# Expert layer: the two slots of a token summed in front of the down-projection

## The chip, the cores and the metric

The kernel runs on one core of one Trainium2 chip. The metric is the device time of one execution in microseconds (us). Lower is better.

## The reference, cut to what matters

One decoder layer on 64 images of 128 tokens and 128 channels: causal self-attention, cross-attention to 77 context tokens, and a mixture of experts with a residual. The change touches only the last part. A token goes to its two best experts of eight ("slots" 0 and 1 here). Each expert differs from the others only by low-rank terms (rank 16, so 8 x 16 = 128 rows for all experts together).

```python
probs = softmax(x @ gate_w.T);  vals, idx = top_k(probs, 2)
rw = vals / sum(vals)                                   # the two gates of a token, w0 + w1 = 1
act_e = silu(x @ w_gate.T + d1_e) * (x @ w_up.T + d3_e) # 512 wide; d1_e, d3_e of rank 16, x2
out = sum_e w_e * act_e @ w_down.T
z_e = act_e @ A2_e.T                                    # 16 wide
out = out + sum_e w_e * (z_e @ B2_e.T) * 2
x = x + out
```

## The kernel before, in words

X holds all 64 images on chip, tokens on the partitions. Three stages follow one another with a layer norm's statistics in front of each: self-attention, cross-attention, `expert_ffn`. Matrix products of the experts are made of three products each of high and low parts in a rounded f32 format (`three`): high x high, high x low, low x high.

**Experts.** `expert_ffn` works on G = 32 groups of NB = 2 images (256 tokens, NT = 256 columns). Each engine runs its own list of steps, `step(g, p)`, one per group, in an order written out by hand; semaphores join them. Every engine executes its own list strictly in order. In step g the engines do, for group g, four units: k = 0, 1 are the halves of the 512 hidden channels for slot 0, k = 2, 3 those for slot 1. Two PSUM banks each (H1, H3) hold the gate and up products of a half; slot 1's products are accumulated on slot 0's, so that its 24 matmuls per unit shrink to 12.

- TensorE (`up`, `down`): `up(g, k)` makes a unit, `down(g, k)` (lines 1793 to 1795) multiplies its result with the down-projection and A2 side by side: the gated activations are the weights, 128 tokens of them at a time, and the 256 columns of w_down and A2 are streamed, so that the outputs have tokens on the partitions. It has 2 x 2 x 3 = 12 matmuls per unit for all four units. Units 2 and 3 of group g-1 are done in step g, as k = -2 and -1. `z_T` (line 1803) transposes the low-rank result of both images, `extra` (lines 1726 to 1728, 6 matmuls of 128 columns) multiplies it with B2. `input_T`, `logits`, `a_products`, `masks` prepare the groups that follow.
- ScalarE: `silu` (1526), `g_hi` (1531, high part of the gated activation), `z_hi` (1536); for the groups that follow `normalise`, `input_T`, `a_hi`, `spread` (one-hot picks widened), `masks` (1504, the two slots' expert masks to SBUF), `gate_odds` (the gates w0 and w1 by a tanh, as [128, 2] each).
- VectorE: `gated` (1640, silu x up, one operand in PSUM), `g_lo` (1645, low part, both operands in SBUF), `x_lo` (1583), `a_lo`, `ranks` and `picks` (top 2 of 8 in small operations), `slot_weights` (1633), `slot_z` (1655, low-rank result times expert mask and gate), `residual_y` (1664, four operations of 128 columns: X + gate x Y), `z_lo` (1671), `residual_z` (1676).
- GpSimd: `slot_sum` (1458, 256 columns) of group g-1, then `slot_inputs` (1466) of group g+1: four products of 512 columns, two for each slot, of the low-rank inputs and the expert mask.
- SyncE stores the two images of a group as soon as `x_done` tells.

The order of VectorE in a step is `residual_z(g-2)`, `x_lo(g+1)`, `ranks(g+1)`, `slot_weights(g)`, `gated 0`, `g_lo 0`, `a_lo(g+1)`, `picks(g+1)`, `gated 1`, `slot_z(g-1)`, `g_lo 1`, `residual_y(g-1)`, `gated 2`, `gated 3`, `z_lo(g-1)`, `g_lo 2`, `g_lo 3`. Of ScalarE it is silu 0, g_hi 0, a_hi, normalise, spread, silu 1, g_hi 1, masks(g+1), silu 2, silu 3, z_hi(g-1), g_hi 2, g_hi 3, input_T(g+2), gate_odds(g+1).

Of the kernel before, what the change touches and what calls it, by code (L numbers as in the profile page):

```python
# [69 lines left out]
def inverse_std(nc, tag, X, ST, MEAN, RSTD, with_stats, load_more=None):  # L70
# [3 lines left out]
    with ctx:  # L74
# [4 lines left out]
        loaded = [ctx.enter_context(nc.semaphore(f"{tag}_loaded{g}")) for g in range(4)]  # L79
# [1254 lines left out]
def expert_ffn(nc, psum, X, MEAN, RSTD, hi, lo, plain, out_dram):  # L1334
# [13 lines left out]
    RANKED, ROUTE = 8, 13  # L1348
    ctx = ExitStack()
    with ctx:  # L1350
# [33 lines left out]
        zt = sb("zt", [128, NB, 2, C])  # L1384
        zz = sb("zz", [128, NB, C])
# [56 lines left out]

        @block.sync
        def _(sp):
            with sp.Fori(0, G) as g:
# [5 lines left out]
            sp.wait_ge(stored, 16 * B)

        @block.gpsimd
        def _(pool):
            def slot_sum(g):
                pool.wait_ge(zt_done, NB * g + NB)
                need(pool, zT_ps, g)
                nc.gpsimd.tensor_tensor(zz[:], zt[:, :, 0, :], zt[:, :, 1, :], ALU.add).then_inc(zz_done, 1)  # L1458

            def slot_inputs(g, p):  # L1460
                pool.wait_ge(mask_sb, g + 1)
                for s in range(2):
                    for part, done in enumerate((ah_done, al_done)):
                        pool.wait_ge(done, g + 1)
                        need(pool, up_ps, UNITS * (g - 2) + 2 * s + 2)
                        nc.gpsimd.tensor_tensor(ZZ[part][:, p, s], AA[part][:].bitcast(F32),  # L1466
                                                M[:, s, :].unsqueeze(1).to_broadcast([C, 2, NT]),
                                                ALU.mult).then_inc(z_done, 1)
# [466 lines left out]
```

## Time and profile before

| | us |
|---|---|
| median of three runs (1767.62 to 1772.02) | 1767.89 |
| profiled execution, its own time | 1771.94 |
| its span, first to last instruction | 1770.1 |
| TensorE busy | 1641.4 (93%) |
| VectorE busy | 1232.2 (70%) |
| ScalarE busy | 924.0 (52%) |
| GpSimd busy | 880.6 (50%) |

Busy times are sums over the whole span; the span of the profiled execution lies 1.8 us below its own time, and that is 4.05 us above the median. The experts' stage starts at 1213.8 us. In its profile one step of the experts repeats with the same order of instructions for all groups but the first and the last, so that one step can be read for all of them. A matmul's duration is longer than its share of the queue, since matmuls are pipelined: what one costs is read from start to start. The same holds, less strongly, for VectorE and ScalarE.

### The profile page before, as it was taken

Reading aid. Unit: us, or ns where it says so; the run is one execution under the profiler, and the core shown is the slowest. Engines: PE = TensorE matmul, PEld = TensorE weight load, DVE = VectorE, ACT = ScalarE, POOL = GpSimd, SP = SyncE. Lnnn points to the kernel's source line nnn. Section 1 sums busy time; section 2 is a strip of 40 time slices with the busy share of each in tenths; the row PEclk is TensorE's granted clock in tenths of the full one; section 3 lists DMA queues with packets and bytes.
Section 4 is the critical chain, followed back from the end, with each engine's and each line's share of the span. In section 5 each row is a group of like instructions: output and inputs, shape, how many; then the busy total and the mean of one; then the engine's idle time right before and its main releaser. Section 6 shows DMA issues by size and latency. Waiting matters only on the chain. (4 is left out here: it accounts for less than half of the span.)

```text
span 1770.1 us, 42709 instructions
## 1 busy us (share of the span) xinstructions
PE 1641.4 (93%) x14274; PEld 1231.9 (70%) x14336; DVE 1232.2 (70%) x2839; ACT 924.0 (52%) x2183; POOL 880.6 (50%) x977
## 2 busy tenths in 40 slices
PE   0899999999977899999999999995999999999998
PEld 0455555555545666666666666555999999999998
DVE  4577777777755667776767767615787887887876
ACT  1345455445443566665666666644545555454453
POOL 0444444444426676776776767621343343443442
PEclk9999999999996899998999989987999999999999
DMA  6000000000000000000000000000000000000000
GB/s 170 2 2 1 1 1 1 1 1 1 1 7 6 4 7 6 7 7 6 7 7 6 7 6 7 2 2 1 8 8 7 9 6 9 9 6 9 9 6 13
DMA packets 26456, 16.60 MB, mean 9 GB/s; under 512 B 6194, under 2 KB 23667, under 8 KB 26355
## 3 DMA queue, kind: packets, MB, share of 16 engines
q1 hardware_dynamic: 26354, 15.29, 3.1%
q8 instruction: 59, 0.97, 0.2%
q14 instruction: 43, 0.34, 0.1%
HBM read 10.03 MB, written 4.19 MB: 8 GB/s over the span
## 5 line engine op out<-in xcount | busy, mean ns | idle before, releaser
L293 ACT ACTIVATE sa_P<-sa_SK 128x1024 f32<-128x1024 f32 x128 | 131.4, 1027 | 150.8 <-PE sa_SK L438 150.8
L1458 POOL TENSOR_TENSOR ff_zz<-ff_zt 128x256 f32<-128x256 f32 x32 | 38.4, 1199 | 319.4 <-DVE ff_zt L1655 319.4
L250 POOL TENSOR_TENSOR sa_KM<-sa_HQK,sc_headmask 128x512 fp32r<-128x512 f32 x64 | 66.6, 1041 | 245.7 <-ACT sa_HQK L288 245.7
L865 ACT ACTIVATE xa_P<-xa_SK 77x1024 f32<-77x1024 f32 x128 | 130.1, 1017 | 98.0 <-PE xa_SK L1157 97.7
L1526 ACT ACTIVATE ff_SG<-bank 128x512 f32<-128x512 f32 x128 | 76.8, 600 | 192.5 <-PE bank L1728 192.5
L1645 DVE TENSOR_TENSOR ff_GL<-ff_GU,ff_GH 128x512 fp32r<-128x512 f32 x128 | 147.7, 1173 | 27.4 <-ACT ff_GH L1531 27.1
L366 DVE TENSOR_REDUCE sa_mx<-sa_SQ 128x8 f32<-128x1024 f32 x128 | 156.6, 1223 | 11.1 <-PE sa_SQ L438 8.3
L1793 PE MATMUL bank<-fh_r,ff_GH 128*128 128x256 f32 x512 | 148.2, 290 | 0.0
L1726 PE MATMUL bank<-ff_ZH,fh_b 128*128 128x256 f32 x512 | 147.8, 289 | 0.0
L791 POOL TENSOR_TENSOR xa_QMH<-xa_QBH,xc_headmask 128x512 fp32r<-128x512 f32 x64 | 72.8, 1138 | 148.2 <-ACT xa_QBH L855 148.1
L1727 PE MATMUL bank<-ff_ZL,fh_b 128*128 128x256 f32 x512 | 145.1, 283 | 0.0
L1728 PE MATMUL bank<-ff_ZH,fl_b 128*128 128x256 f32 x512 | 145.0, 283 | 0.0
L1795 PE MATMUL bank<-fh_r,ff_GL 128*128 128x256 f32 x512 | 143.5, 280 | 0.0
L750 POOL TENSOR_TENSOR xa_E<-xa_E 128x1232 f32<-128x1232 f32 x64 | 143.2, 2238 | 0.0
L1794 PE MATMUL bank<-fl_r,ff_GH 128*128 128x256 f32 x512 | 142.9, 279 | 0.0
L1640 DVE TENSOR_TENSOR ff_GU<-ff_SG,bank 128x512 f32<-128x512 f32 x128 | 88.0, 687 | 68.9 <-ACT ff_SG L1526 63.5
L1531 ACT CAST ff_GH<-ff_GU 128x512 fp32r<-128x512 f32 x128 | 78.9, 623 | 55.3 <-DVE ff_GU L1640 32.2
L1466 POOL TENSOR_TENSOR ff_ZH<-ff_AH,ff_M 128x512 fp32r<-128x512 f32 x64 | 83.7, 1308 | 41.5 <-ACT ff_M L1504 41.5
L962 DVE TENSOR_REDUCE xa_FEAT<-xa_SQ 128x12 f32<-128x924 f32 x64 | 71.7, 1120 | 41.8 <-PE xa_SQ L1106 41.6
L457 PE MATMUL sa_SK<-sa_shift,sa_pick_row 128*128 128x512 f32 x256 | 99.7, 470 | 0.2 <-ACT sa_P L293 0.2
L1726 PEld LDWEIGHTS bank<-ff_ZH,fh_b 128*128 128x128 f32 x512 | 98.5, 192 | 0.0
L1727 PEld LDWEIGHTS bank<-ff_ZL,fh_b 128*128 128x128 f32 x512 | 98.5, 192 | 0.0
(259 smaller groups left out, 5381.2 us busy)
## 6 DMA issues: line engine op xcount, KB each, us to landing
xa_shift<-xa_row SPq DMA_DIRECT2D x256, 2.0 KB
out<-X SPq DMA_DIRECT2D x64, 64.0 KB, 1.5
xa_cx<-ctx SPq DMA_DIRECT2D x64, 38.5 KB
sa_shift<-sa_mT SPq DMA_DIRECT2D x64, 8.0 KB, 1.8
fr_b<-L_ffn_B SPq DMA_DIRECT2D x2, 256.0 KB, 3.9
fr_r<-down_a SPq DMA_DIRECT2D x1, 512.0 KB, 4.7
fr_w<-L_ffn_w_gate SPq DMA_DIRECT2D x1, 256.0 KB, 3.5
fr_w<-L_ffn_w_up SPq DMA_DIRECT2D x1, 256.0 KB, 3.6
```

The source lines that it names most:

```text
L293: nc.scalar.activation(P[:, 2 * (k % 2) + h, :], SK[:], ACT.Exp).then_inc(p_ready, 1)
L366: nc.vector.tensor_reduce(mx[:, p, 2 * JH * h:2 * JH * h + 2 * JH], SQ[:].rearrange("q (j k) -> q j k", k=T), AX.X, ALU.max).then_inc(max_ ...
L457: mm(bank(SK, a), pick_row[:], shift[:, k % 2, JH * g:JH * g + JH, :].rearrange("c j t -> c (j t)"), start=True, stop=False)
L750: nc.gpsimd.tensor_tensor(E2[:], E1[:, b % 2], E1[:, b % 2], ALU.mult).then_inc(e2_ready, 1)
L865: nc.scalar.activation(P[0:TC, (2 * b + h) % 4, :], SK[0:TC, :], ACT.Exp).then_inc(p_ready, 1)
L1645: nc.vector.tensor_tensor(GG[1][:, k % 4, :], GU[:, k % 2, :], GG[0][:, k % 4, :].bitcast(F32), ALU.subtract).then_inc(gl_done, 1)
L1726: mm(out, w[0], x[0], start=start, stop=False, **kw)
L1727: mm(out, w[0], x[1], start=False, stop=False, **kw)
L1728: return mm(out, w[1], x[0], start=False, stop=stop, **kw)
L1793: mm(out, h, RD[0][:, f, :], start=(s == 0 and f == 0), stop=False, skip_group_check=True)
L1794: mm(out, h, RD[1][:, f, :], start=False, stop=False, skip_group_check=True)
L1795: last = mm(out, l, RD[0][:, f, :], start=False, stop=(s == 1 and f == 3), skip_group_check=True)
```

## The change

The sum of a token's two slots is taken on the gated activations, w0 (act0 + (w1/w0) act1), so that the down-projection proper runs once for both; w0 is applied at the residual. The low-rank part needs the slots apart by expert: PZ holds A2 x act0 and A2 x (act0 + ratio x act1), and the masks ME = (mask1, mask0 + mask1 - mask0) pick out the parts, whose difference goes on. The matrices are now the weights and the activations (256 tokens) are streamed, so outputs have channels on the partitions and are transposed back at the end (`back_T`).

TensorE: `down` has 6 matmuls of 256 columns for k = 0, 1 and 12 for k = 2, 3; `extra` has 3 of 256 columns; `z_T` is gone; `ratios` (two f32 products of 128 columns, which lay the ratio across the partitions) and `back_T` (two transposes) are new. ScalarE: `ratio_copy` and `out_copy` are new, `z_hi` moves between silu 2 and silu 3. VectorE: `odds` (reciprocal and product, [128, 2]), two `slot_sum` of 512 columns, two `z_parts` of 256 columns, two `residual` of 128 columns in place of `slot_weights`, `slot_z`, `residual_y` and `residual_z`; `z_lo` reads SBUF alone and stands in front of `gated 2`. GpSimd: two `scaled` of 512 columns (silu of slot 1 times the ratio, in place), which `gated` 2 and 3 wait for, two `output_masks` and a `z_sum` of 256 columns, and `slot_inputs` of slot 0 stands in front of `z_sum`.

```diff
-def slot_inputs(g, p):
+def slot_inputs(g, p, s):
     pool.wait_ge(mask_sb, g + 1)
...
+def output_masks(g, p):
+    pool.wait_ge(mask_sb, g + 1)
+    need(pool, zb_done, 2 * (g - 1))
+    nc.gpsimd.tensor_tensor(ME[:, p, 1], M[:, 0, :], M[:, 1, :], ALU.add).then_inc(me_done, 1)
+    pool.wait_ge(me_done, 2 * g + 1)
+    nc.gpsimd.tensor_tensor(ME[:, p, 0], ME[:, p, 1], M[:, 0, :], ALU.subtract).then_inc(me_done, 1)
+def scaled(g, u):
+    pool.wait_ge(rb_sb, g + 1)
+    pool.wait_ge(silu_done, UNITS * g + 2 + u + 1)
+    unit2 = SG[:, u, :].rearrange("f (c n) -> f c n", c=2)
+    nc.gpsimd.tensor_tensor(unit2, unit2, RB[:].unsqueeze(1).to_broadcast([128, 2, NT]),
+                            ALU.mult).then_inc(scaled_done, 1)
+def z_sum(g):
+    pool.wait_ge(zb_done, 2 * g + 2)
+    need(pool, zl_done, g)
+    nc.gpsimd.tensor_tensor(zs[:], zb[:, 1, :], zb[:, 0, :], ALU.subtract).then_inc(zs_done, 1)
 def step(g, p):
+    if real(g + 1):
+        slot_inputs(g + 1, 1 - p, 0)
     if real(g - 1):
-        slot_sum(g - 1)
+        z_sum(g - 1)
+    scaled(g, 0)
+    scaled(g, 1)
     if real(g + 1):
-        slot_inputs(g + 1, 1 - p)
+        slot_inputs(g + 1, 1 - p, 1)
+        output_masks(g + 1, 1 - p)
...
+def ratio_copy(g):
+    act.wait_ge(rb_ps, g + 1)
+    need(act, scaled_done, 2 * g)
+    nc.scalar.copy(RB[:], BF[:, NT:2 * NT]).then_inc(rb_sb, 1)
 def silu(g, k):
     act.wait_ge(up_ps, UNITS * g + k + 1)
...
     nc.scalar.activation(SG[:, k % 2, :], H1[k % 2][:], ACT.Silu).then_inc(silu_done, 1)
 def g_hi(g, k):
-    act.wait_ge(gu_done, UNITS * g + k + 1)
+    if k < 2:
+        act.wait_ge(gu_done, UNITS * g + k + 1)
+    else:
+        act.wait_ge(sum_done, 2 * g + k - 1)
     need(act, y_ps, UNITS * g + k - 3)
-    nc.scalar.copy(GG[0][:, k % 4, :], GU[:, k % 2, :]).then_inc(gh_done, 1)
+    nc.scalar.copy(GG[0][:, k, :], GU[:, k % 2, :]).then_inc(gh_done, 1)
 def z_hi(g):
-    act.wait_ge(zT_ps, g + 1)
-    need(act, extra_ps, g)
-    nc.scalar.copy(ZT[0][:], BS[:, 0:NT]).then_inc(zh_done, 1)
+    act.wait_ge(zs_done, g + 1)
+    need(act, out_ps, g)
+    nc.scalar.copy(ZT[0][:], zs[:]).then_inc(zh_done, 1)
+def out_copy(g):
+    act.wait_ge(out_ps, g + 1)
+    need(act, back_ps, g)
+    nc.scalar.copy(OT[:], OUT[:, 0:NT]).then_inc(out_sb, 1)
 def step(g, p):
     silu(g, 0)
...
         normalise(g + 2)
     if real(g + 1):
         spread(g + 1)
+    ratio_copy(g)
     silu(g, 1)
     g_hi(g, 1)
     if real(g + 1):
         masks(g + 1)
     silu(g, 2)
-    silu(g, 3)
     if real(g - 1):
         z_hi(g - 1)
+    silu(g, 3)
+    if real(g + 2):
+        input_T(g + 2, p)
+    if real(g - 1):
+        out_copy(g - 1)
     g_hi(g, 2)
     g_hi(g, 3)
-    if real(g + 2):
-        input_T(g + 2, p)
     if real(g + 1):
-        gate_odds(g + 1, 1 - p)
+        gate_odds(g + 1)
...
+def odds(g):
+    dve.wait_ge(w0_ready, g + 1)
+    nc.vector.reciprocal(w0_inv[:], W0[:, bass.ds(NB * g, NB)]).then_inc(inv_ready, 1)
+    dve.wait_ge(inv_ready, g + 1)
+    dve.wait_ge(w1_ready, g + 1)
+    need(dve, rb_ps, g)
+    nc.vector.tensor_tensor(ratio[:], w1[:], w0_inv[:], ALU.mult).then_inc(ratio_ready, 1)
 def gated(g, k):
-    dve.wait_ge(silu_done, UNITS * g + k + 1)
+    if k < 2:
+        dve.wait_ge(silu_done, UNITS * g + k + 1)
+    else:
+        dve.wait_ge(scaled_done, 2 * g + k - 1)
     need(dve, gl_done, UNITS * g + k - 1)
-    nc.vector.tensor_tensor(GU[:, k % 2, :], SG[:, k % 2, :], H3[k % 2][:], ALU.mult).then_inc(gu_done, 1)
+    out = GU if k < 2 else G1
+    nc.vector.tensor_tensor(out[:, k % 2, :], SG[:, k % 2, :], H3[k % 2][:], ALU.mult).then_inc(gu_done, 1)
+def slot_sum(g, u):
+    dve.wait_ge(gu_done, UNITS * g + 2 + u + 1)
+    nc.vector.tensor_tensor(GU[:, u, :], GU[:, u, :], G1[:, u, :], ALU.add).then_inc(sum_done, 1)
 def g_lo(g, k):
     dve.wait_ge(gh_done, UNITS * g + k + 1)
     need(dve, y_ps, UNITS * g + k - 3)
-    nc.vector.tensor_tensor(GG[1][:, k % 4, :], GU[:, k % 2, :], GG[0][:, k % 4, :].bitcast(F32),
+    nc.vector.tensor_tensor(GG[1][:, k, :], GU[:, k % 2, :], GG[0][:, k, :].bitcast(F32),
                             ALU.subtract).then_inc(gl_done, 1)
-def slot_z(g, p):
+def z_parts(g, p):
     dve.wait_ge(y_ps, UNITS * g + UNITS)
...
+    dve.wait_ge(me_done, 2 * g + 2)
+    need(dve, zs_done, g)
+    for part in range(2):
+        nc.vector.tensor_tensor(zb[:, part, :], PZ[:, part * NT:(part + 1) * NT], ME[:, p, part],
+                                ALU.mult).then_inc(zb_done, 1)
 def z_lo(g):
     dve.wait_ge(zh_done, g + 1)
...
+    need(dve, out_ps, g)
+    nc.vector.tensor_tensor(ZT[1][:], zs[:], ZT[0][:].bitcast(F32), ALU.subtract).then_inc(zl_done, 1)
+def residual(g):
+    dve.wait_ge(back_ps, g + 1)
+    for n in range(NB):
+        xb = X[:, bass.ds((NB * g + n) * C, C)]
+        nc.vector.scalar_tensor_tensor(xb, OUT[:, NT + n * C:NT + (n + 1) * C], W0[:, bass.ds(NB * g + n, 1)], xb,
+                                       ALU.mult, ALU.add).then_inc(x_done, 1)
 def step(g, p):
     if real(g - 2):
-        residual_z(g - 2)
+        residual(g - 2)
+    odds(g)
     if real(g + 1):
         x_lo(g + 1, 1 - p)
         ranks(g + 1)
-    slot_weights(g, p)
     gated(g, 0)
     g_lo(g, 0)
     if real(g + 1):
         a_lo(g + 1)
         picks(g + 1)
     gated(g, 1)
-    if real(g - 1):
-        slot_z(g - 1, 1 - p)
     g_lo(g, 1)
     if real(g - 1):
-        residual_y(g - 1, 1 - p)
+        z_parts(g - 1, 1 - p)
+        z_lo(g - 1)
     gated(g, 2)
+    slot_sum(g, 0)
     gated(g, 3)
-    if real(g - 1):
-        z_lo(g - 1)
+    slot_sum(g, 1)
     g_lo(g, 2)
     g_lo(g, 3)
...
+def ratios(g):
+    pe.wait_ge(ratio_ready, g + 1)
+    if real(g + 1):
+        pe.wait_ge(route, ROUTE * (g + 1) + 1)
+    for n in range(NB):
+        last = mm(BF[:, NT + n * T:NT + (n + 1) * T], ratio[:, n:n + 1].to_broadcast([128, 128]), ident[:],
+                  start=True, stop=True, skip_group_check=True)
+    last.then_inc(rb_ps, 1)
 def down(g, k):
-    if not unit(g, k):
+    if not real(g):
         return
-    s, u = divmod(k % UNITS, 2)
+    u = k % 2
     pe.wait_ge(gl_done, UNITS * g + k + 1)
     if k == 0:
-        need(pe, zt_done, NB * g)
-        need(pe, y_step, 4 * g)
+        need(pe, zb_done, 2 * g)
+    if k == 2:
+        need(pe, x_done, NB * g)
     for c in range(2):
         f = 2 * u + c
...
+        unit = [t[:, k, c * NT:(c + 1) * NT] for t in GG]
+        at = k // 2 * NT
+        last = three(PZ[:, at:at + NT], [t[:, f, C:2 * C] for t in RD], unit, f == 0, f == 3, skip_group_check=True)
+        if k >= 2:
+            last = three(OUT[:, 0:NT], [t[:, f, 0:C] for t in RD], unit, f == 0, False, skip_group_check=True)
     last.then_inc(y_ps, 1)
...
 def extra(g):
     pe.wait_ge(zh_done, g + 1)
     pe.wait_ge(zl_done, g + 1)
+    last = three(OUT[:, 0:NT], [t[:] for t in B2], [t[:] for t in ZT], False, True, skip_group_check=True)
+    last.then_inc(out_ps, 1)
+def back_T(g):
+    pe.wait_ge(out_sb, g + 1)
     for n in range(NB):
-        last = three(BS[:, NT + n * C:NT + (n + 1) * C],
-                     [t[:, n * T:(n + 1) * T] for t in ZT], [t[:] for t in B2], True, True)
-    last.then_inc(extra_ps, 1)
+        last = tr(OUT[:, NT + n * C:NT + (n + 1) * C], OT[:, n * T:(n + 1) * T], ident[:])
+    last.then_inc(back_ps, 1)
 def step(g, p):
     up(g, 0, p)
-    down(g, -2)
+    down(g - 1, 2)
     if real(g + 1):
         a_products(g + 1, 1 - p)
+    ratios(g)
     up(g, 1, p)
-    down(g, -1)
     if real(g + 1):
         masks(g + 1)
+    down(g - 1, 3)
     up(g, 2, p)
     up(g, 3, p)
-    if real(g - 1):
-        z_T(g - 1)
-    down(g, 0)
     if real(g + 2):
         input_T(g + 2)
-    down(g, 1)
+    down(g, 0)
     if real(g - 1):
         extra(g - 1)
+    down(g, 1)
     if real(g + 2):
         logits(g + 2)
+    if real(g - 1):
+        back_T(g - 1)
```

## Rows read from the trace of the kernel before

**Rows 1.** Page: the span; part 1, busy us, share and count of each engine.
```profile
span 1770.1 us, 42709 instructions
...
PE 1641.4 (93%) x14274; PEld 1231.9 (70%) x14336; DVE 1232.2 (70%) x2839; ACT 924.0 (52%) x2183; POOL 880.6 (50%) x977
```

**Rows 2.** Time windows: length, busy us (count) of each engine, granted clock.
```profile
484.00:528.00 44.00, 34.53 (x341) 19.71 (x341) 25.75 (x63) 18.53 (x37) 12.85 (x16) 0.94 0.02 5
528.00:572.00 44.00, 34.77 (x148) 24.58 (x148) 22.03 (x42) 15.74 (x51) 25.69 (x34) 0.59 0.02 7
1475.60:1492.40 16.80, 16.80 (x147) 16.76 (x145) 13.39 (x34) 8.55 (x19) 6.68 (x6) 1.00 0.03 8
```

**Rows 3.** Chain of waits, experts stage: start us, us, what.
```profile
1257.22 0.39 PE bank L1740 x4
...
1727.62 0.39 PE bank L1740 x4
```

**Rows 4.** Timeline of TensorE, experts: start us, us, engine, line, what.
```profile
1474.84 0.22 PE L1726 MATMUL bank<-fh_b,ff_ZTH 128*128 128x128 f32 x1
...
1475.45 0.56 PE L1740 MATMUL bank<-fc_gw,ff_xT 128*128 128x8 f32 x4
...
1478.82 0.28 PE L1793 MATMUL bank<-fh_r,ff_GH 128*128 128x256 f32 x1
...
1480.22 0.28 PE L1726 MATMUL bank<-ff_XH,fh_a 128*128 128x256 f32 x1
```

**Rows 5.** Timeline of TensorE in cross-attention: one f32 product, then another's start.
```profile
707.54 0.49 PE L1092 MATMUL xa_M<-xa_xcT,xc_wq 128*128 128x128 f32 x2
707.87 0.34 PE L1093 MATMUL xa_M<-xa_xcT,xc_wk 128*128 128x77 f32 x2
```

**Rows 6.** Timeline of VectorE, one step; in brackets idle before it, releaser.
```profile
1476.61 0.41 DVE L1676 TENSOR_TENSOR X<-X,bank 128x256 f32 x1
1476.94 0.41 DVE L1583 TENSOR_TENSOR ff_XL<-ff_xT,ff_XH 128x256 fp32r<-128x256 f32 x1
...
1479.21 0.17 DVE L1633 TENSOR_TENSOR ff_V<-ff_pick,ff_wt 128x16 f32<-128x16 f32 x1
...
1479.82 0.69 DVE L1640 TENSOR_TENSOR ff_GU<-ff_SG,bank 128x512 f32<-128x512 f32 x1 [0.34 <-ACT ff_SG L1526]
...
1485.42 0.75 DVE L1655 TENSOR_TENSOR ff_zt<-bank,ff_V 128x256 f32<-128x256 f32 x2
1486.19 0.69 DVE L1645 TENSOR_TENSOR ff_GL<-ff_GU,ff_GH 128x512 fp32r<-128x512 f32 x1
1486.80 1.25 DVE L1664 SCALAR_TENSOR_TENSOR X<-bank,ff_wt,X 128x128 f32 x4
...
1490.15 3.31 DVE L1645 TENSOR_TENSOR ff_GL<-ff_GU,ff_GH 128x512 fp32r<-128x512 f32 x2
```

**Rows 7.** Timeline of ScalarE, the same step.
```profile
1479.10 0.60 ACT L1526 ACTIVATE ff_SG<-bank 128x512 f32<-128x512 f32 x1 [4.20 <-PE bank L1728]
...
1485.97 0.58 ACT L1504 CAST ff_M<-bank 128x512 f32<-128x512 bf16 x1
```

**Rows 8.** Timeline of GpSimd, the same step.
```profile
1486.25 1.22 POOL L1458 TENSOR_TENSOR ff_zz<-ff_zt 128x256 f32<-128x256 f32 x1 [10.12 <-DVE ff_zt L1655]
1487.44 1.29 POOL L1466 TENSOR_TENSOR ff_ZH<-ff_AH,ff_M 128x512 fp32r<-128x512 f32 x1
1488.68 1.30 POOL L1466 TENSOR_TENSOR ff_ZL<-ff_AL,ff_M 128x512 fp32r<-128x512 f32 x1
...
1491.20 1.72 POOL L1466 TENSOR_TENSOR ff_ZL<-ff_AL,ff_M 128x512 fp32r<-128x512 f32 x1
```

**Rows 9.** Timeline of VectorE, last step of the experts.
```profile
1757.28 1.28 DVE L1645 TENSOR_TENSOR ff_GL<-ff_GU,ff_GH 128x512 fp32r<-128x512 f32 x2
```

**Rows 10.** Groups of instructions, shapes apart: count, busy us, mean ns, idle before.
```profile
L256 POOL TENSOR_TENSOR sa_QML<-sa_LQK,sc_headmask 128x512 fp32r<-128x512 f32 x64 | 66.6, 1041 | 0.0
...
L375 DVE RECIPROCAL sa_rinv<-sa_R 128x16 f32<-128x16 f32 x64 | 15.9, 248 | 4.9 <-PE sa_R L498 4.9
```

More of the change, by code:

```diff
@@ L78, in inverse_std @@
         t = ctx.enter_context(nc.sbuf_tensor(tag + "_t", [128, B], F32))
-        loaded = [ctx.enter_context(nc.semaphore(f"{tag}_loaded{g}")) for g in range(4)]
+        loaded = [ctx.enter_context(nc.semaphore(f"{tag}_loaded{g}")) for g in range(4 if with_stats is not None else 0)]
         gathered = ctx.enter_context(nc.semaphore(tag + "_gathered"))
@@ L1383, in expert_ffn @@
         GG = [sb("GH", [128, 4, 2 * NT], F32R), sb("GL", [128, 4, 2 * NT], F32R)]
[L1384 to L1385 removed]
+        G1 = sb("G1", [128, 2, 2 * NT])
+        zb = sb("zb", [128, 2, NT])
+        zs = sb("zs", [128, NT])
+        OT = sb("OT", [C, NT])
         ZT = [sb("ZTH", [C, NT], F32R), sb("ZTL", [C, NT], F32R)]
@@ L1400, in expert_ffn @@
         th_ready = sem("th_ready")
-        wt_ready = sem("wt_ready")
-        v_ready = sem("v_ready")
+        w0_ready = sem("w0_ready")
+        w1_ready = sem("w1_ready")
+        inv_ready = sem("inv_ready")
+        ratio_ready = sem("ratio_ready")
+        rb_ps = sem("rb_ps")
+        rb_sb = sem("rb_sb")
+        scaled_done = sem("scaled_done")
+        sum_done = sem("sum_done")
+        me_done = sem("me_done")
         mask_ps = sem("mask_ps")
@@ L1445, in _ @@
             with sp.Fori(0, G) as g:
-                sp.wait_ge(x_done, g + 1)
+                sp.wait_ge(x_done, NB * g + NB)
                 for n in range(NB):
@@ L1454, in _ @@
         def _(pool):
[L1455 to L1458, printed above, removed]
-            def slot_inputs(g, p):
-                pool.wait_ge(mask_sb, g + 1)
[L1462 to L1468, printed above, removed]
+            def slot_inputs(g, p, s):
+                pool.wait_ge(mask_sb, g + 1)
+                for part, done in enumerate((ah_done, al_done)):
+                    pool.wait_ge(done, g + 1)
+                    need(pool, up_ps, UNITS * (g - 2) + 2 * s + 2)
+                    nc.gpsimd.tensor_tensor(ZZ[part][:, p, s], AA[part][:].bitcast(F32),
+                                            M[:, s, :].unsqueeze(1).to_broadcast([C, 2, NT]),
+                                            ALU.mult).then_inc(z_done, 1)
@@ L1473, in step, with first @@
                 if real(g + 1):
-                    slot_inputs(g + 1, 1 - p)
-            groups(pool, lambda: slot_inputs(0, 0), step, lambda: slot_sum(G - 1))
+                    slot_inputs(g + 1, 1 - p, 1)
+                    output_masks(g + 1, 1 - p)
+            def first():
+                slot_inputs(0, 0, 0)
+                slot_inputs(0, 0, 1)
+                output_masks(0, 0)
+            groups(pool, first, step, lambda: z_sum(G - 1))
         @block.scalar
@@ L1710, in end @@
             def end():
-                residual_z(G - 2)
-                slot_z(G - 1, 1)
-                residual_y(G - 1, 1)
+                residual(G - 2)
+                z_parts(G - 1, 1)
                 z_lo(G - 1)
-                residual_z(G - 1)
-                dve.wait_ge(x_done, G)
+                residual(G - 1)
+                dve.wait_ge(x_done, NB * G)
             groups(dve, first, step, end)
@@ L1745, in a_products @@
                 pe.wait_ge(xl_ready, g + 1)
-                need(pe, x_done, g - 2)
                 for m in range(2):
@@ L1844, in end @@
             def end():
-                down(G, -2)
-                down(G, -1)
-                z_T(G - 1)
+                down(G - 1, 2)
+                down(G - 1, 3)
                 extra(G - 1)
+                back_T(G - 1)
             groups(pe, first, step, end)
```

83 lines of the change are left out of this document (21 added, 62 removed).

## The prediction

> **What bounds the kernel now.** I read the page's busy shares first: TensorE is busy 93% of the span, the next engine 70% [rows 1]. Over a whole span that says little, so I went to the window of one step in the experts' stage: TensorE is busy 16.80 of 16.80 us at full clock, VectorE 13.39, ScalarE 8.55, GpSimd 6.68 [rows 2]. The chain of waits confirms the period: the same piece of TensorE's work returns at 1257.22 and at 1727.62, 470.4 us or 28 steps of 16.80 [rows 3]. So the experts' stage is bound by TensorE's queue, and each step has slack of 3.4 us on VectorE. How that slack is made up is in the timelines. They show no spare room that is free of waits: VectorE works its list in order, and stands before `gated 0` only 0.34 us [rows 6].
>
> **TensorE's part, alone.** Twelve matmuls of one old `down` take from 1478.82 to 1480.22, 1.40 us or 0.117 each [rows 4]. `down` goes from 48 to 36 of them: -1.40 us. `extra` takes 0.61 us for its 6 matmuls of 128 columns [rows 4]; 3 of 256 columns take 0.35: -0.26. `z_T` is replaced by `back_T`, two transposes for two: 0. `ratios` is new: one f32 product of 128x128 takes 0.33 us from start to start [rows 5], two take +0.66. Sum -1.0 us, a period of 15.8 us, if nothing else held TensorE.
>
> **What the port costs.** In the old step `g_lo 2` and `g_lo 3` together take 3.31 us while GpSimd's products run, and 1.28 in the last step, where GpSimd has none [rows 6, 9]. One of them, in the queue, is 0.61 us: `g_lo 1` from 1486.19 to 1486.80 [rows 6]. GpSimd pays as well: its product beside them takes 1.72 where an undisturbed one goes from 1487.44 to 1488.68, 1.24 [rows 8]. And its `slot_sum`, starting at 1486.25, just behind `g_lo 1`, and ending where the next begins at 1487.44, moved only once `g_lo 1` was through at 1486.80: its own work is 0.64 us [rows 6, 8]. All of it fits turns taken instruction by instruction. From 1490.15 the pair waits for the product until 1491.20, runs 0.61, waits for the next product's 1.24, runs 0.61: 3.51 against 3.31 shown. `gated`, with an operand in PSUM, does not pay. The Trainium skill (SBUF — State Buffer, "Who interferes with whom") states the rule: a VectorE instruction with two SBUF inputs and a GpSimd instruction that reads SBUF exclude each other for a whole instruction. It speaks against this change, which adds such instructions on both sides; a shared bandwidth instead would stretch both and leave no turns.
>
> GpSimd's own work in a step grows from 4 x 1.24 + 0.64 = 5.6 to 4 + 2 products of 1.24 and three operations of 0.64, 9.4 us. For the products I take 1.24 also for `scaled`; another such product elsewhere takes 1.04 [rows 10], which is the low bound. The Trainium skill (GPSIMD Engine Reference, "Elementwise — side-by-side cycle accounting") gives 2.6 cycles an element for two inputs, an estimate of 1.1 us for 512; with it the forecast would be about 9 us lower. VectorE gains two `slot_sum` of 0.61 with both operands in SBUF, and `z_lo` becomes one of them too.
>
> **The ring.** What decides is order. VectorE runs its list strictly in order, GpSimd too, and the change makes them wait for each other three times in a step. I walk from the start of `gated 0` of one step to that of the next.
> - A: `gated 0` to the first product of GpSimd. Between are g_hi 0, g_lo 0, picks, spread, silu 1, gated 1, g_hi 1 and the copy of the masks, which GpSimd's whole list for the step waits for. Before, `gated 0` starts at 1479.82 [rows 6] and the copy ends at 1486.55 [rows 7]: 6.7, with 0.1 for the handoff 6.8 us. (A handoff: the silu ends at 1479.70, `gated 0` starts at 1479.82 [rows 6, 7].) `ratio_copy` adds work on ScalarE in front of silu 1, but silu 1 waited for TensorE there before; taken as 0.
> - B: GpSimd's chain, with VectorE's turns between. Two products for slot 0, 2.48. Then only `z_sum`, 0.64. `z_parts` (0.75, as `slot_z` [rows 6]) was ready long before and lies beside the products. z_hi (ScalarE) and then `z_lo` (VectorE) come behind `z_sum`, and in the meantime GpSimd has begun `scaled 0`, 1.24: `z_lo` gets the port after it, 0.33 (as `residual_z`, 1476.61 to 1476.94 [rows 6]). All of VectorE's list stands behind that `z_lo`: it is idle from the end of `z_parts` for some 3.5 us. Then in turn: `scaled 1` 1.24 (`gated 2` beside it), slot sum 0.61, product 1.24 (`gated 3` beside it), slot sum 0.61, product 1.24, g_lo 2 0.61, an output mask 0.64, g_lo 3. Sum without the last: 7.44 + 1.28 + 0.33 + 1.83 = 10.9 us.
> - C: g_lo 3 0.61, `residual` 2 x 0.31 (four such took 1.25 [rows 6]), `odds` 0.45 (a reciprocal of 16 columns took 0.25 [rows 10], a [128, 16] product 0.17 [rows 6]), `x_lo` and `ranks` 2.27 (1476.94 to 1479.21 [rows 6]). Sum 3.95 us. The old V products are gone from here.
>
> A + B + C = 21.7 us a step, against 16.8. TensorE with 15.8 us of work has 5.9 us of idle time in it and its own waits lie inside: in front of `down` of the last group's unit 2 it waits for `residual` (x_done, which stands behind g_lo 3), and before `extra` for `z_lo`. With `extra` waiting, unit 1's `down`, `logits`, `back_T` and the next group's first `up` stand behind it, but that `up` ends some 2 us before the ring needs its silu. ScalarE's silu 3 stands behind z_hi, which costs nothing as `scaled 1` waits for the port anyway. The stores on SyncE follow `x_done` and are hidden as before, but for the last.
>
> **The sum.** 31 periods between the first and the last `gated 0`, each 4.9 us longer: +152. The first step has no low-rank result of a group before it (-1), the last step's chain of slot sum, z_sum, z_hi, z_lo, extra, copy and transpose is longer by about as much: 0. The profiled execution took 1771.94 us by its own time, 1.8 more than its span of 1770.1 [rows 1]; so 1924, and as it lies 4.05 above the median of the three runs, 1920 against 1767.89.
>
> **Bounds of this case.** `scaled` at 1.04 and everything else of GpSimd's 256 columns in proportion: 0.6 less a step, 1901. If each of some twelve handoffs of 0.12 us shows behind the turns: +1.4 a step, 1963.
>
> **Rivals.**
> 1. *The order binds, but the port does not, or only in part.* For it: turns may fall luckier than I walk them. Against it: g_lo's pair at 3.31 us in the steps with GpSimd and 1.28 without [rows 6, 9]. Then B shrinks: s0 and z_sum end at 9.8 us, scaled 0 and gated 2 at 11.8, gated 3 at 13.0, the second slot sum 13.65, g_hi 3, g_lo 3 at 15.1, rest of C 3.35: 18.5 us a step, 31 x 1.7 = +53, 1821. Mixed cases lie up to 1900.
> 2. *Faster: TensorE stays the bound.* Place: TensorE's queue from `up 0` to `up 0`. Price: 15.8 instead of 16.8 us, 32 steps, -32: 1736. It decides only if the ring of the two other engines closes in under 15.8 us. For it: TensorE is the bound now and its work does shrink. Against: even without the port the ring takes 18.5.
> 3. *The clock falls.* Now a step runs at clock 1.00. TensorE would stand idle in stretches of up to 2.7 us, 5.9 of each 21.7. In cross-attention's start, with 34.77 us busy of 44, the clock was 0.59; just before it with 34.53 of 44 it was 0.94 [rows 2]. So both can be had near such shares. At 1.2 GHz a step of matmuls would take some 31 us, which closes the gaps again; half of the steps so gives 26.6 us, +304, 2072.
> 4. *No change in time*, the ring closing at 16.8 just as TensorE's work did: only a coincidence of 1 and 2.
>
> **How the numbers follow.** Ring with turns, 1901 to 1963: 0.72. Rival 1: 0.15. Rival 2: 0.06. Rival 3: 0.05. Rival 4: 0.02. The likeliest gives 1920. The range takes in its bounds and most of rival 1: 1835 to 1965. What a measurement here can tell from no change is about 0.3%, 5 us. Faster by more than that 0.06, same 0.02, slower 0.92.
>
> **What would show it.** A period of 21 to 22.5 us between the same instructions of two steps. In VectorE's timeline an idle stretch of 3 us or more before `z_lo`, ended by ScalarE's z_hi, itself behind GpSimd's `z_sum`; slot sums of more than 1 us and a `g_lo 2` near 1.8; GpSimd busy without a hole from the masks' copy to the output masks; TensorE busy near three quarters, with waits for X and for ZTL; the window's clock at 1.00. Wrong would be: `z_lo` without idle time before it, TensorE busy throughout, or slot sums of 0.69 beside running `scaled` (then the port is not what I take it for).

## The result and the profile after

The changed kernel takes 1902.95 us (median of four runs, 1900.55 to 1908.83) against 1768.88 for the kernel of before beside it: a ratio of 1.076, 95% interval 1.073 to 1.079. Slower, inside the range of 1835 to 1965, 17 us under the 1920 forecast. The last of the reordered kernels (experiments 6 to 10 below) brings the same arithmetic to 1760.34 us, 0.5% under the kernel of before, which took 1768.21 beside it.

The page first. Beside [rows 1], TensorE's share fell from 93% to 87%, and the chain of waits, which was TensorE's alone through the experts, is now spread over VectorE, ScalarE, GpSimd and the handoffs between them ("issue" is time in which an engine waited for nothing that the profile shows). The third line below is that chain of waits, as shares of the span.

```profile
span 1900.8 us, 42609 instructions
...
PE 1652.0 (87%) x13984; PEld 1224.2 (64%) x13984; DVE 1267.8 (67%) x2775; ACT 943.2 (50%) x2247; POOL 1033.0 (54%) x1105
...
issue 12%; DVE 12%; ACT 4%; PE 3%; POOL 2%; DVEq 1%; ACTq 0%; POOLq 0%
```

Windows of the experts' stage (as [rows 2]: length, busy us (count) of TensorE, its weight loads, VectorE, ScalarE, GpSimd, granted clock, DMA share, GB/s):

```profile
1276.40:1297.30 20.90, 15.89 (x133) 15.36 (x132) 14.51 (x31) 9.15 (x21) 11.26 (x10) 1.00 0.03 7
1351.20:1372.80 21.60, 19.49 (x134) 19.27 (x134) 14.49 (x32) 9.26 (x21) 11.43 (x9) 0.80 0.02 6
1519.40:1540.40 21.00, 17.04 (x144) 16.52 (x143) 14.52 (x31) 9.23 (x21) 11.49 (x9) 1.00 0.02 6
1255.00:1856.00 601.00, 491.46 (x3810) 476.88 (x3809) 417.79 (x890) 261.90 (x601) 331.39 (x260) 0.94 0.02 6
```

VectorE's timeline over one step, from `gated 0` at 1519.43 to the next at 1540.42, 20.99 us; it stands beside [rows 6]. To be seen: 2.98 us idle in front of `z_lo` (ZTL), slot sums (L1695) of 1.07 and 1.08, the pair of `g_lo` at 2.92 (1.78 and 1.21, which overlap by 0.08).

```profile
1519.43 0.69 DVE L1691 TENSOR_TENSOR ff_GU<-ff_SG,bank 128x512 f32<-128x512 f32 x1 [0.22 <-DVE ff_rank L1659]
...
1526.22 0.75 DVE L1709 TENSOR_TENSOR ff_zb<-bank,ff_ME 128x256 f32<-128x256 f32 x2
1529.95 0.95 DVE L1715 TENSOR_TENSOR ff_ZTL<-ff_zs,ff_ZTH 128x256 fp32r<-128x256 f32 x1 [2.98 <-ACT ff_ZTH L1576]
1530.83 0.67 DVE L1691 TENSOR_TENSOR ff_G<-ff_SG,bank 128x512 f32<-128x512 f32 x1
1531.54 1.07 DVE L1695 TENSOR_TENSOR ff_GU<-ff_GU,ff_G 128x512 f32<-128x512 f32 x1
1532.53 0.67 DVE L1691 TENSOR_TENSOR ff_G<-ff_SG,bank 128x512 f32<-128x512 f32 x1
1533.24 1.08 DVE L1695 TENSOR_TENSOR ff_GU<-ff_GU,ff_G 128x512 f32<-128x512 f32 x1
1534.23 2.92 DVE L1700 TENSOR_TENSOR ff_GL<-ff_GU,ff_GH 128x512 fp32r<-128x512 f32 x2
1537.08 0.59 DVE L1721 SCALAR_TENSOR_TENSOR X<-bank,ff_W,X 128x128 f32 x2
...
1540.42 0.69 DVE L1691 TENSOR_TENSOR ff_GU<-ff_SG,bank 128x512 f32<-128x512 f32 x1 [0.21 <-DVE ff_rank L1659]
```

GpSimd's timeline of the same step (beside [rows 8]): from the masks' copy to the output mask it has no hole. Undisturbed products start 1.27 and 1.24 apart; the two that alternate with slot sums take 1.69 and 1.73 from their own start to that of the next.

```profile
1526.16 1.31 POOL L1469 TENSOR_TENSOR ff_ZH<-ff_AH,ff_M 128x512 fp32r<-128x512 f32 x1 [9.33 <-ACT ff_M L1538]
1527.43 1.28 POOL L1469 TENSOR_TENSOR ff_ZL<-ff_AL,ff_M 128x512 fp32r<-128x512 f32 x1
1528.67 0.74 POOL L1491 TENSOR_TENSOR ff_zs<-ff_zb 128x256 f32<-128x256 f32 x1
1529.37 2.69 POOL L1485 TENSOR_TENSOR ff_SG<-ff_SG,ff_RB 128x512 f32<-128x512 f32 x2
1532.02 1.74 POOL L1469 TENSOR_TENSOR ff_ZH<-ff_AH,ff_M 128x512 fp32r<-128x512 f32 x1
1533.71 1.75 POOL L1469 TENSOR_TENSOR ff_ZL<-ff_AL,ff_M 128x512 fp32r<-128x512 f32 x1
1535.44 1.17 POOL L1477 TENSOR_TENSOR ff_ME<-ff_M 128x256 f32<-128x256 f32 x1
```

The waits of the whole run (who waited for whom, us in total, times, longest) name the chain through `z_sum`, z_hi and `z_lo`, and TensorE behind it:

```profile
DVE ff_ZTL L1715 <- ACT ff_ZTH L1576: 90.6, 32, 3.0
...
ACT ff_ZTH L1576 <- POOL ff_zs L1491: 65.5, 32, 7.6
...
PE bank L1770 <- DVE ff_ZTL L1715: 56.4, 32, 2.6
...
PE bank L1770 <- DVE X L1721: 41.0, 27, 3.4
```

**Where the time is.** The first `gated 0` starts at 1227.91, the last at 1872.46: 31 steps of 20.79 us. Before, 1230.45 and 1747.78 give 16.69. That is 31 x 4.10 = 127 us. The tail behind the last `gated 0` is 28.3 us against 22.3, the start 2.5 shorter: 127 + 6.0 - 2.5 = 130.7, the whole difference of the spans (1900.8 and 1770.1). The 2.5 us are not the change's: cross-attention, whose code is the same, ends 2.6 us earlier in this execution (1201.2 and 1203.8). In the twelve profiled executions of this document the first `gated 0` starts anywhere from 1220.2 to 1234.2 us, so a difference of a few us between two executions is better read from the steps than from the totals.

The steps of the changed kernel are not all alike. Most take 20.8 to 20.9 us; four, with a mean clock of 0.80, take 21.5 to 21.6 (1351.2 to 1372.8 is one). Steps at a clock of 0.92 take no more than those at 1.00. So the clock cost some 3 of the 127 us.

### The profile page after: what moved, and what is told of

Same layout as the page of the kernel before. It is cut to its first block and busy times, and to the rows that moved or that the text cites. A ratio compares the mean times of both kernels' runs of the same rounds, so it can differ in the third digit from the quotient of the medians.

```text
span 1900.8 us, 42609 instructions
## 1 busy us (share of the span) xinstructions
PE 1652.0 (87%) x13984; PEld 1224.2 (64%) x13984; DVE 1267.8 (67%) x2775; ACT 943.2 (50%) x2247; POOL 1033.0 (54%) x1105
## 5 line engine op out<-in xcount | busy, mean ns | idle before, releaser
L1469 POOL TENSOR_TENSOR ff_ZH<-ff_AH,ff_M 128x512 fp32r<-128x512 f32 x64 | 96.9, 1515 | 320.9 <-ACT ff_M L1538 320.9
L1700 DVE TENSOR_TENSOR ff_GL<-ff_GU,ff_GH 128x512 fp32r<-128x512 f32 x128 | 135.9, 1080 | 53.1 <-ACT ff_GH L1571 34.3
L1770 PE MATMUL bank<-ff_GH,fh_r 128*128 128x256 f32 x384 | 117.8, 307 | 42.3 <-DVE X L1721 41.0
L1771 PE MATMUL bank<-ff_GL,fh_r 128*128 128x256 f32 x384 | 110.2, 287 | 0.0
L1772 PE MATMUL bank<-ff_GH,fl_r 128*128 128x256 f32 x384 | 110.2, 287 | 0.0
L1770 PEld LDWEIGHTS bank<-ff_GH,fh_r 128*128 128x128 f32 x384 | 74.3, 194 | 47.6 <-DVE ff_GL L1700 29.4
L1772 PEld LDWEIGHTS bank<-ff_ZH,fl_b 128*128 128x128 f32 x512 | 99.8, 195 | 0.0
```

What stands on the lines that cost most here:

```text
L1700: nc.vector.tensor_tensor(GG[1][:, k, :], GU[:, k % 2, :], GG[0][:, k, :].bitcast(F32), ALU.subtract).then_inc(gl_done, 1)
L1770: mm(out, w[0], x[0], start=start, stop=False, **kw)
L1771: mm(out, w[0], x[1], start=False, stop=False, **kw)
L1772: return mm(out, w[1], x[0], start=False, stop=stop, **kw)
```

## The experiments

"After" means the changed kernel; differences are to its 1903 us.

**1. z_lo later.** VectorE's wait moved behind the second slot sum:

```diff
                     z_parts(g - 1, 1 - p)
-                    z_lo(g - 1)
                 gated(g, 2)
                 slot_sum(g, 0)
                 gated(g, 3)
                 slot_sum(g, 1)
+                if real(g - 1):
+                    z_lo(g - 1)
```

> VectorE's z_lo is moved behind the second slot sum, so that nothing of VectorE's list stands behind it while it waits for GpSimd and ScalarE. In the changed kernel VectorE idles 2.9 us a step in front of z_lo. Theory A (the ring of GpSimd's chain): gated 2 waits for scaled 0, which ends at about the same moment as z_lo does now, so the idle time moves in front of gated 2 and the step stays at 20.9 us or gains 0.5 for one more turn at the port: 1900 to 1925 us. Theory B (the wait of z_lo itself is what costs): 2.9 us a step less, 31 steps, about 1815 us.

Measured 2016.73 us, 114 more. VectorE's timeline:

```profile
1519.53 0.69 DVE L1691 TENSOR_TENSOR ff_GU<-ff_SG,bank 128x512 f32<-128x512 f32 x1 [1.91 <-ACT ff_SG L1563]
...
1531.38 0.69 DVE L1691 TENSOR_TENSOR ff_G<-ff_SG,bank 128x512 f32<-128x512 f32 x1 [3.68 <-POOL ff_SG L1485]
...
1534.71 1.48 DVE L1715 TENSOR_TENSOR ff_ZTL<-ff_zs,ff_ZTH 128x256 fp32r<-128x256 f32 x1
1538.28 1.29 DVE L1700 TENSOR_TENSOR ff_GL<-ff_GU,ff_GH 128x512 fp32r<-128x512 f32 x2 [2.08 <-ACT ff_GH L1571]
...
1544.32 0.69 DVE L1691 TENSOR_TENSOR ff_GU<-ff_SG,bank 128x512 f32<-128x512 f32 x1 [1.21 <-ACT ff_SG L1563]
```

The idle time did move: `gated 2` now starts 11.85 us behind `gated 0` (11.40 before) and is released by GpSimd's `scaled`. That part is as theory A had it, and theory B falls. What A's number left out is the queue behind another wait: ScalarE has `out_copy` in front of g_hi 2 and 3, `out_copy` waits for `extra`, and `extra` for `z_lo`. ScalarE's timeline shows the copy of OT at 1537.36, and both high parts only behind it:

```profile
1537.36 0.37 ACT L1581 COPY ff_OT<-bank 128x256 f32<-128x256 f32 x1 [5.53 <-PE bank L1773]
1537.62 1.14 ACT L1571 CAST ff_GH<-ff_GU 128x512 fp32r<-128x512 f32 x2
```

VectorE's pair of `g_lo` waits 2.08 us for them. From the pair's end to the next `gated 0` it takes 1.4 us more than after as well: `gated 0` waits 1.21 us for silu 0, and that for TensorE. The step of these rows takes 24.79 us, the mean one 24.34. So the time lies far outside both theories' numbers, 92 us over the top of A's range. TensorE's clock fell as well, to a mean of 0.90 over the run and 0.79 to 0.86 in nearly every step; how much of the 114 us is its doing was not separated.

**2. z_sum and scaled first on GpSimd.** The same nine operations:

```diff
-                if real(g + 1):
-                    slot_inputs(g + 1, 1 - p, 0)
                 if real(g - 1):
                     z_sum(g - 1)
                 scaled(g, 0)
                 scaled(g, 1)
                 if real(g + 1):
+                    slot_inputs(g + 1, 1 - p, 0)
                     slot_inputs(g + 1, 1 - p, 1)
```

> GpSimd's order becomes z_sum, scaled 0, scaled 1, then the four products and the output masks; nothing else changes, its work is the same. Theory A (GpSimd's chain in its order is in the ring): z_sum may start when z_parts ends, 7.6 us after gated 0 in place of 9.2, everything behind it comes 1.3 to 1.6 us earlier: 19.4 us a step, about 1858 us. Theory C (GpSimd's sum of work or the port's turns bind, order does not): no change, 1903 us.

Measured 1912.97 us: 10 more, 55 over theory A's number and 10 over theory C's. VectorE's timeline:

```profile
1523.24 0.60 DVE L1720 SCALAR_TENSOR_TENSOR X<-bank,ff_W,X 128x128 f32 x2
...
1524.92 0.56 DVE L1649 TENSOR_TENSOR ff_above<-ff_lg 128x64 f32<-128x64 f32 x1
...
1525.54 0.76 DVE L1649 TENSOR_TENSOR ff_above<-ff_lg 128x64 f32<-128x64 f32 x1
...
1527.62 0.69 DVE L1690 TENSOR_TENSOR ff_GU<-ff_SG,bank 128x512 f32<-128x512 f32 x1 [0.22 <-DVE ff_rank L1658]
...
1536.47 0.98 DVE L1714 TENSOR_TENSOR ff_ZTL<-ff_zs,ff_ZTH 128x256 fp32r<-128x256 f32 x1 [1.38 <-ACT ff_ZTH L1575]
...
1540.78 3.46 DVE L1699 TENSOR_TENSOR ff_GL<-ff_GU,ff_GH 128x512 fp32r<-128x512 f32 x2
```

Up to the last `g_lo` theory A is right: `z_lo` starts 8.85 us behind `gated 0` instead of 10.52, and the pair ends at 16.5 (1527.62 to 1544.16) instead of 17.65. But GpSimd's last product and its two output masks come later by it, and now run beside `odds` and `ranks`. There even operations of 64 columns pay: 0.56 and 0.76 us where 0.22 is usual, each through with the output mask beside it. GpSimd's rows of the masks:

```profile
1524.41 0.99 POOL L1477 TENSOR_TENSOR ff_ME<-ff_M 128x256 f32<-128x256 f32 x1
1525.48 0.74 POOL L1479 TENSOR_TENSOR ff_ME<-ff_ME,ff_M 128x256 f32<-128x256 f32 x1
```

From the pair's end to the next `gated 0` it takes 4.4 us instead of 3.3. The gain is given back at the same port: the step is 20.91 us, as after.

The 10 us more are another matter. But for the first two and the last, steps at full clock take 20.9 us throughout; seven steps, each with a mean clock of 0.92, take 22.2 to 22.4. In such a step silu 2 waits for TensorE 2.54 us instead of 1.04, GpSimd's `scaled 0` waits for silu 2, and all behind it comes 1.46 us later: seven times, 10 us. Two neighbouring steps as windows, then their silu 2 on ScalarE:

```profile
1337.10:1358.00 20.90, 16.59 (x136) 15.77 (x135) 16.31 (x32) 9.26 (x21) 11.76 (x9) 1.00 0.02 6
1358.00:1380.30 22.30, 17.75 (x134) 17.02 (x134) 16.54 (x32) 9.15 (x21) 11.77 (x9) 0.92 0.02 6
```

```profile
1344.20 0.60 ACT L1562 ACTIVATE ff_SG<-bank 128x512 f32<-128x512 f32 x1 [1.04 <-PE bank L1771]
...
1366.59 0.60 ACT L1562 ACTIVATE ff_SG<-bank 128x512 f32<-128x512 f32 x1 [2.54 <-PE bank L1771]
```

**3. The slot sum's operand in PSUM.** `gated` 2 and 3 write over the gate products; `up` then waits for the slot sum before it reuses the bank:

```diff
-                out = GU if k < 2 else G1
-                nc.vector.tensor_tensor(out[:, k % 2, :], SG...
+                out = GU[:, k % 2, :] if k < 2 else H1[k % 2][:]
+                nc.vector.tensor_tensor(out, SG...
...
-                nc.vector.tensor_tensor(GU[:, u, :], GU[:, u, :], G1[:, u, :], ALU.add)
+                nc.vector.tensor_tensor(GU[:, u, :], GU[:, u, :], H1[u][:], ALU.add)
```

> gated 2 and 3 write their product in place of the gate products in PSUM, and the slot sum reads it there: the slot sums then have one operand in SBUF, as many operations as before. Theory A with turns at the port: a slot sum takes 0.69 us in place of 1.06, GpSimd's two products beside them 1.3 in place of 1.7; the chain is shorter by 0.7 to 1.0 us a step: 1872 to 1881 us. Without a port in it (only GpSimd's and VectorE's own lengths): no change, 1903 us.

Measured 1870.7 us: 32 less, 1 us under the forecast range. VectorE's and then GpSimd's timeline: the slot sums (L1695) take 0.69, the products beside them start 1.23 apart, the step is 20.00 us.

```profile
1502.32 0.69 DVE L1691 TENSOR_TENSOR ff_GU<-ff_SG,bank 128x512 f32<-128x512 f32 x1 [0.22 <-DVE ff_rank L1659]
...
1514.36 0.69 DVE L1695 TENSOR_TENSOR ff_GU<-ff_GU,bank 128x512 f32<-128x512 f32 x1
...
1515.69 0.69 DVE L1695 TENSOR_TENSOR ff_GU<-ff_GU,bank 128x512 f32<-128x512 f32 x1
...
1522.32 0.69 DVE L1691 TENSOR_TENSOR ff_GU<-ff_SG,bank 128x512 f32<-128x512 f32 x1 [0.21 <-DVE ff_rank L1659]
```

```profile
1514.82 1.29 POOL L1469 TENSOR_TENSOR ff_ZH<-ff_AH,ff_M 128x512 fp32r<-128x512 f32 x1
1516.05 1.31 POOL L1469 TENSOR_TENSOR ff_ZL<-ff_AL,ff_M 128x512 fp32r<-128x512 f32 x1
```

Same operations, same lengths of work, one operand elsewhere: the port is shown, for the two slot sums alone. The mean step is 19.83 us against 20.79, 30 us in all; the other 2 of the 32 lie within what the start of the experts varies by.

**4 and 5. More work for TensorE.** The transposes back six times over in the changed kernel, `z_T` six times over in the kernel of before (`for _ in range(6):` around each).

> TensorE makes the two transposes back six times over, with the same result: some 1.1 us a step more in its queue. Theory A (ring of VectorE, ScalarE and GpSimd, TensorE has room): no change, 1900 to 1908 us. If TensorE's queue binds after all (its work, or its clock of 0.84 to 0.92 in many steps): 1.1 us x 32 = +35, 1938 us.

> The control of the run with more transposes: in the kernel of before, z_T makes its two transposes six times over, with the same result, some 1.1 us a step more in TensorE's queue. There TensorE binds, so it should show in full: 32 x 1.1 = +35, 1800 to 1808 us. If it cost nothing here either, added transposes would be no measure of who binds.

Measured 1902.33 us (0.6 less than after) and 1806.69 (37 more than the 1770.06 of the kernel of before beside it; its steps take 17.89 us where they took 16.80). The added work is in the trace of the first, 1.51 us for twelve:

```profile
1513.39 1.51 PE L1861 MATMUL bank<-fc_ident,ff_OT 128*128 128x128 f32 x12
```

So TensorE binds before and has room after. Run 4 also shows the clock from another side: with ten more transposes a step its mean over the experts (1255 to 1856) is 0.99 instead of 0.94, no step lies under 0.92, and the four steps of 21.5 us are gone.

**6 to 10. Other orders.** Operations as in experiment 3 (in the third of them, as in the changed kernel), the four lists permuted; the mask products and output masks are issued one by one. VectorE's list in the first of them:

```diff
-residual odds x_lo ranks gated0 g_lo0 a_lo picks gated1 g_lo1 z_parts z_lo gated2 slot_sum0 gated3 slot_sum1 g_lo2 g_lo3
+gated0 residual odds ranks picks z_parts gated1 x_lo g_lo0 g_lo1 z_lo a_lo gated2 slot_sum0 g_lo2 gated3 slot_sum1 g_lo3
```

> The changed kernel with the slot sum read from PSUM and all four engines' lists put in another order, the same operations: VectorE has ranks and picks of the next group and z_parts in the gaps where it waited for ScalarE, GpSimd does z_sum and scaled 0 first, TensorE makes U1, the downs and the ratios before U2. Walked with the durations of the rows a step closes at 16.1 to 16.5 us, now with TensorE nearly full (its own work 15.8): 1903 - 31 x 4.5 = about 1765 us, between 1750 and 1780. Theory A (order and port made the loss, not the joined slots as such): that time. Theory D (the work added on VectorE and GpSimd is itself too much, whatever the order): no step under 18.5, over 1830 us.

> Another order of the same lists, with ScalarE's high part of unit 0 behind silu 1 and odds first on VectorE; walked with the rows' durations 15.9 to 16.4 us a step: 1745 to 1775 us. It tells whether one walk's order was luck: Theory A expects it within 15 us of the other order, Theory D over 1830 us.

> The same order as the first reordered kernel, but the slot sums read both operands from SBUF as in the changed kernel: the port's part alone in the new order. Walked, a step is 0.4 to 0.5 us longer: +13 to +16 us on that kernel's time. If the port did not matter any more in this order: the same time within 5 us.

Measured 1765.1 (ratio to before 0.9986, interval 0.9962 to 1.0011), 1779.54 (1.0054), and 1786.63 us with the slot sums from SBUF. Theory D falls: the work fits into a step. The third run is the cleanest measure of the order: it has the changed kernel's own operations and operands, and takes 1786.63 us instead of 1902.95. The order alone is worth 116 of the 134 us. Which of the moves does it was not separated; the two single moves that were tried (experiments 1 and 2) gained nothing.

What the slot sums' operand is worth on top of it is 21.5 us by the medians, but the steps say less: 16.89 against 16.42 us, 14.4 us in all, as walked (13 to 16). Of the 24 us between the two profiled executions 9 lie ahead of the experts, where the code is the same (cross-attention ends at 1207.6 and 1198.2). The second order is 5 us outside its own forecast, 14 from the first. Then:

> A fourth order of the same operations, from what the first reordered kernel's trace shows: there TensorE still waits 0.2 us for x_lo and 0.2 for the transposes back, and each g_lo pays the port. x_lo goes in front of ranks, extra in front of unit 0's down, ScalarE copies the outputs in front of silu 3. Walked with the rows' durations 15.8 to 16.2 us a step: 0 to 0.4 less than there, 1753 to 1765 us, ratio to the kernel of before 0.990 to 0.998. If the walk has reached what it can tell (a few tenths a step), 1765 to 1780 as the two before it.

> The same as the run beside it but for four neighbours changed (normalise in front of g_hi 0, g_hi 1 in front of the ratio's copy, x_lo in front of odds, an output mask in front of slot 1's products): walked, no difference. Measured within 5 us of it if such neighbours do not matter.

Measured 1762.95 us (0.997, interval 0.9946 to 0.9994) and 1760.34 (0.995, interval 0.9932 to 0.9968), both as forecast. The second differs from the first in two more neighbours than its text says: g_hi 2 in front of `gate_odds`, `logits` in front of `back_T`. It beats both kernels, by 8 us in the case of the kernel of before: its steps are 0.52 us shorter (16.17 against 16.69), its tail 5 us longer. It is the best of four orders tried, and its profile is of the fastest of its twelve executions (1750.61 us). Its window, behind that of the first reordered kernel:

```profile
1255.00:1700.00 445.00, 431.60 (x3584) 420.59 (x3583) 360.08 (x837) 244.84 (x567) 295.22 (x242) 1.00 0.03 8
```

```profile
1255.00:1700.00 445.00, 438.25 (x3649) 425.22 (x3648) 382.58 (x850) 249.82 (x579) 302.97 (x247) 1.00 0.03 8
```

The order of the best one (names as in the lists ahead; group in brackets where it isn't g):

```
TensorE: up0 up1 down2(g-1) down3(g-1) ratios up2 a_products(g+1) masks(g+1) up3 input_T(g+2) extra(g-1) down0 down1 logits(g+2) back_T(g-1)
ScalarE: silu0 normalise(g+2) g_hi0 silu1 g_hi1 ratio_copy spread(g+1) silu2 z_hi(g-1) a_hi(g+1) masks(g+1) input_T(g+2) out_copy(g-1) silu3 g_hi2 gate_odds(g+1) g_hi3
VectorE: residual(g-2) gated0 x_lo(g+1) odds ranks(g+1) gated1 z_parts(g-1) picks(g+1) g_lo0 g_lo1 z_lo(g-1) a_lo(g+1) gated2 slot_sum0 gated3 slot_sum1 g_lo2 g_lo3
GpSimd:  z_sum(g-1) scaled0 products(g+1, slot 0) scaled1 mask(g+1) product(g+1, slot 1) mask(g+1) product(g+1, slot 1)
```

TensorE is busy 98% of its window, at clock 1.00. VectorE's timeline repeats after 16.24 us, not 15.8: `z_lo` takes 1.51 us instead of some 0.4, held at the port behind GpSimd's `scaled 0`, and TensorE's `extra` waits for it (the last row below; it starts 0.51 us behind the matmul before it, of which some 0.4 is waiting). Without that wait TensorE's queue would close in about 15.8. `gated 3` still waits 1.76 us for GpSimd.

```profile
1501.48 1.51 DVE L1730 TENSOR_TENSOR ff_ZTL<-ff_zs,ff_ZTH 128x256 fp32r<-128x256 f32 x1
...
1517.72 1.51 DVE L1730 TENSOR_TENSOR ff_ZTL<-ff_zs,ff_ZTH 128x256 fp32r<-128x256 f32 x1
...
1522.92 0.70 DVE L1706 TENSOR_TENSOR bank<-ff_SG,bank 128x512 f32<-128x512 f32 x1 [1.76 <-POOL ff_SG L1493]
```

```profile
1503.14 0.36 PE L1788 MATMUL bank<-ff_ZTH,fh_b 128*128 128x256 f32 x1 [0.24 <-DVE ff_ZTL L1730]
```

## Why the prediction was right, step by step

- **TensorE bound before, not after:** shown by runs 4 and 5. Its own 15.8 us a step is borne out by the best order: 16.24, less some 0.4 of waiting, is about 15.8. One term of the sum was too large: I took 0.33 us for one f32 product of 128 columns from [rows 5]; `ratios` takes 0.36 us for both (1519.94 to 1520.30), and the matmul behind it 0.08 longer. TensorE had room, so this moved nothing.
- **A, `gated 0` to GpSimd's first product:** 6.8 forecast, 6.73 measured (1519.43 to 1526.16). `ratio_copy` cost nothing there, as taken: silu 1 waited 0.43 us for TensorE before, and not at all now.
- **B with the last g_lo:** 11.5 forecast, 10.92 measured (1526.16 to 1537.08). This is the term that was mis-sized. I had a product and a VectorE instruction beside it take 1.24 + 0.61 us in turn. The rows give 1.11 + 0.59: the first slot sum runs from 1531.54 to 1532.61, 0.59 past the product's start at 1532.02, and the product's successor starts at 1533.71, 1.10 after the slot sum's end. Over the 62 such pairs of the run that last piece is 1.10 to 1.13, median 1.11. So VectorE's instruction keeps its whole turn, and 0.13 us of GpSimd's instruction pass beside it; why was not tested. Over five turns this is 0.65 us a step. The pair in [rows 6] fits it too: 1490.15 to 1491.20 waiting, then 0.6, 1.11 and 0.6 come to 3.3, where my turns gave 3.51.
- **C without that g_lo:** 3.34 forecast, 3.34 measured (1537.08 to 1540.42).
- **The step:** +4.9 forecast, +4.10 as a mean. Of the 0.8 between them B is 0.57 and A 0.07; the sum of the terms was 21.63, taken as 21.7; and the mean steps differ by 0.09 less than the steps of the rows.
- **The ends:** 0 forecast, +3.5 measured: the tail 6.0 longer, less the 2.5 of an earlier start that are chance.
- **The 17 us too many** are thus not B alone, but a sum of errors of both signs: 25 too many by the steps, 3.5 too few at the ends, and 4 too few because the profiled execution of before lay 4.05 above its median and that of after 0.4 below.
- **The port as exclusive turns:** as the Trainium skill has it (SBUF — State Buffer, "Who interferes with whom"), and the traces agree: moving one operand to PSUM took the stretch off both engines. GpSimd loses 0.45 us to an instruction that takes 0.59 of the port, by the 0.13 above.
- **Rival 1 (order without port)** was a part and not a rival: at 18.5 us a step it lay under experiment 3's 20.0, where three of the turns at the port were left. By experiment 9 the order is the larger part of the loss, the slot sums' port the smaller. **Rival 2** did not happen in the changed order and nearly happens in the last one. **Rival 3, the clock:** it dipped, which I had as unlikely in any form, to a mean of 0.80 in four steps and 0.92 to 0.97 in twelve others, and cost some 3 us here. In experiment 2 it cost 10, so room on TensorE is no full protection.
- Of the signs named, the wait before `z_lo` (2.98), slot sums over 1 us, a `g_lo 2` near 1.8 (1.78), GpSimd without a hole and TensorE busy three quarters (15.89 of 20.90) were seen. The period, 20.79 as a mean, lies just under the 21 to 22.5 named, and a clock of 1.00 holds only in part of the steps.

## What to carry to other kernels

When the bound engine is relieved, walk one step of the others' lists in order, with the handoffs, before counting what was saved: here TensorE gave back 1 us of its own work a step, and a ring of three engines made the step 4 longer. The same operations in another order took 116 us less, so a loss like this one speaks against the order before it speaks against the change. A wait put at the end of a chain across two engines costs what stands behind it, and moving it can expose a longer one (experiment 1); look at every queue on the way. Where VectorE and GpSimd both work from SBUF, an operand left in PSUM frees both, and which small operations run beside the long ones counts as much as their sum.

## What had not been expected of the hardware

- TensorE's clock fell to 0.80 over a step (1351.2 to 1372.8) and 0.94 on average, while its longest wait in that step was 2.11 us, and the clock was 1.00 in other steps of the same pattern (1276.4 to 1297.3), with waits of 1.69, 1.96 and 1.36. What tells such steps apart was not found. Ten more transposes a step (run 4) brought the average to 0.99.
- A clock that falls on an engine with room can still cost: in experiment 2 a step at 0.92 takes 1.46 us more, in the changed kernel one at 0.92 takes nothing more and one at 0.80 takes 0.7. In the rows the cost comes by a silu that waits longer for TensorE; where in the step the clock is low is likely to decide, which was not tested.
- VectorE's operations of 64 columns, 0.22 us alone, took 0.56 and 0.76 beside GpSimd's output masks (experiment 2).
- VectorE writing its product into a PSUM bank while reading another took 0.68 us, where into SBUF it took 0.67 (experiment 3; the changed kernel).
- A GpSimd product that alternates with a VectorE instruction of two SBUF inputs ends 1.11 us after it, though its own work is 1.24.
